# Cross-attention's probabilities x values with three heads per stationary operand, and the last weight's units moved behind the loop

## The chip, the cores and the metric

One core of a Trainium2 chip runs the whole kernel. The metric is the device time of one launch in microseconds; shown are the median and the extremes of three runs, and one further execution that the hardware profiler recorded. The engines are TensorE (PE; PEld is its load of stationary operands), VectorE (DVE), ScalarE (ACT), GpSimd (POOL) and SyncE (SP), whose queue issues nearly all DMAs.

## What is computed

A perceiver block on 64 latent tokens of width 256: cross-attention to 6272 context tokens (32 heads of 8), self-attention with 16 heads of 128 whose weights come as codes times block scales, and a mixture-of-experts FFN.

```python
x = x + xattn(layernorm(x), ctx, Wq, Wk, Wv)         # q and k rms-normalised per head of 8
x = x + attn(layernorm(x), wq, wk, wv, wo, biases)   # w = codes * repeat(scales, 32, axis=0)
x = x + ffn(layernorm(x), gate, shared, experts)     # top 2 of 8 experts, and a shared one
# inside xattn, per head:
scores = einsum('bhnd,bhmd->bhnm', q, k) * 8 ** -0.5
out = einsum('bhnm,bhmd->bhnd', softmax(scores), v)
```

## The kernel before

**The loop.** The context is cut into 49 tiles of 128 tokens. Each engine runs `step` once per tile, with the stages staggered over tiles. For tile t TensorE does `scores(t, half)` for two halves of 16 heads (L736, 16 matmuls, two heads each), then `values(t - 1, half)` (L750), then the keys and values of tile t + 5 (L772, six matmuls with 512 columns in fp32r, as high and low parts). ScalarE takes the exponentials of each half (L394, 128x1024 into `probs`), and the squares, logarithm and power for the keys' norm (L406, L412, L416). VectorE splits the context, sums the squares, copies the values out of PSUM (L544), scales the keys (L552) and writes their parts (L560). GpSimd makes the context's low part (L348) and the keys' last part (L354). There is no maximum in the softmax: the exponentials and, through a column of ones, their sums are accumulated over all tiles in PSUM.

**Probabilities x values.** `v_sb` holds for every pair of heads a stationary operand of 17 columns: 8 + 8 value columns and one column of ones (L327 sets the ones). Its moving operand is the 128 probabilities of the pair (2 heads x 64 tokens), so each product has two useful and two useless quarters. The 16 matmuls of a tile go to four column groups of TensorE in turn (PSUM partitions 0, 32, 64, 96), four 128-column regions each, all in PSUM bank 6. All operands are f32. `pv_done` counts two per tile.

**After the loop.** VectorE copies the 128x512 sums (L567), TensorE transposes them in eight pieces (L781), VectorE takes reciprocals (L569), multiplies by them (L572), adds the residual (L576), and the second layernorm follows (L456 to L471). TensorE fills the time with `keep_busy(16)` (L695), transposes the normalised rows (L687), waits for both `ring_free` semaphores and starts the projections (L793).

**The quantised weights.** Sixteen units of 128x1024: twelve of Wq, Wk, Wv, four of Wo. `load_codes(u)` brings the codes (512 KB, L280) into their final place, `load_scales(u)` the scales (256 KB for the first twelve, L286; 512 KB for Wo's, L289) into a ring of two slots, after `ring_free` says that unit u - 2 has been multiplied. GpSimd's `dequantise(u)` (L340) multiplies in place and increments `ring_free`. With `DEQ = 3`, SP issues one unit every third tile and GpSimd multiplies one every third tile: the sixteenth is in the loop's last steps. TensorE's gate ahead of the projections asks for all of them:

```python
for k in range(RING):
    pe.wait_ge(ring_free[k], UNITS // RING + 1)
```

**SP's queue.** SP goes through one list in order: per step the transposing DMA of a finished tile's keys (`turn`, L277, after `k2_done`), the next context tile (L269), and at their steps a unit's codes and scales; behind the last step `load_round(r)` for the FFN's five rounds (704 KB, L294, and 352 KB, L295), which the last stage waits for (`up_in`, `down_in`).

Of the kernel before, what the change touches and what calls it, by code (L numbers as in the profile page):

```python
# [19 lines left out]
ALU = mybir.AluOpType  # L20
# [86 lines left out]
def wait(engine, semaphore, count):  # L107

    if count is not None:
        engine.wait_ge(semaphore, count)  # L110


def perceiver(nc, x, ctx_t, xwq, xwkv, codes, scales, wo_scales, qkv_bias, bo, gate_w, gate_bias,
              up_w, down_w, eye, expert_ids, pair_heads, out):
    with ExitStack() as stack:
        def sb(name, shape, dt=F32):
            return stack.enter_context(nc.sbuf_tensor(name, shape, dt))
# [41 lines left out]
        v_flat = sb("v_flat", [P, 8 * PAIRS * VW])  # L159
        v_sb = v_flat[:].rearrange("p (s r v) -> p s r v", s=8, r=PAIRS)  # L160
# [18 lines left out]
        o_sb = sb("o_sb", [P, CG * P])  # L179
        o_den = sb("o_den", [N, 2, PAIRS])  # L180
        o_cat = sb("o_cat", [N, PAIRS, 2, XD])
        x1 = sb("x1", [N, D])
        x1b, x2 = q_f, q_sq

# [31 lines left out]
        ps_o = ps[:, 6, :]  # L216
        ps_oT = ps[0:N, 0:2, :].rearrange("p s (r v) -> p s r v", v=CT)
# [41 lines left out]
        @block.sync  # L259
        def _(sp):  # L260
            sp.dma_start(x_sb[:], x).then_inc(ready("x_in"), 16)
            sp.dma_start(wkv_f[:], xwkv).then_inc(ready("wkv_in"), 16)

            def load(t):

                if t >= 4:
                    sp.wait_ge(ctx_hi_done, t - 3)
                    sp.wait_ge(ctx_lo_done, t - 3)
                sp.dma_start(ctx_f[:, t % 4], ctx_t[t]).then_inc(ctx_in[t % 4], 16)  # L269

            def turn(t):

                sp.wait_ge(k2_done, t + 1)
                if t >= 4:
                    sp.wait_ge(scores_mm, 2 * t - 6)
                rows = k12[:, t % 4].rearrange("p r w -> p (r w)")
                sp.dma_start_transpose(kT[:, t % 4], rows).then_inc(keys_in[t % 4], 16)  # L277

            def load_codes(u):
                sp.dma_start(w_all[:, u], codes[:, u]).then_inc(codes_in[u % RING], 16)  # L280

            def load_scales(u):

                sp.wait_ge(ring_free[u % RING], u // RING + 1)
                if u < NQKV:
                    sp.dma_start(s_ring[:, u % RING, 0:512], scales[u].unsqueeze(0).to_broadcast(  # L286
                        [P // NB, NB, 512])).then_inc(scales_in[u % RING], 16)
                else:
                    sp.dma_start(s_ring[:, u % RING], wo_scales[u - NQKV].unsqueeze(0).to_broadcast(  # L289
                        [QB, P // QB, WS])).then_inc(scales_in[u % RING], 16)  # L290

            def load_round(r):

                sp.dma_start(up_sb[:, :, r], up_w[:, :, r]).then_inc(ready("up_in"), 16)  # L294
                sp.dma_start(dn_sb[:, r], down_w[:, r]).then_inc(ready("down_in"), 16)  # L295

            small = ((bias_t[:], qkv_bias), (bo_sb[:], bo.to_broadcast([N, D])), (gate_sb[:], gate_w),
                     (gb_sb[:], gate_bias.to_broadcast([P, E])))

            for t in range(2):  # L300
                load(t)
            sp.dma_start(wq_sb[:], xwq).then_inc(ready("wq_in"), 16)
            for t in range(2, T + LAG):
                if t >= LAG:
                    turn(t - LAG)
                if t < T:
                    load(t)
                u, piece = divmod(t - LAG, DEQ)
                if 0 <= u < UNITS and piece == 0:
                    load_codes(u)  # L310
                if 0 <= u < UNITS and piece == 1:
                    load_scales(u)
                if 2 <= t < 2 + len(small):
                    dst, src = small[t - 2]
                    sp.dma_start(dst, src).then_inc(ready("small_in"), 16)
            for r in range(NR):
                load_round(r)
            sp.wait_ge(ready("y"), 1)
            sp.dma_start(out, x_sb[:]).then_inc(ready("out_written"), 16)
            sp.wait_ge(ready("out_written"), 16)  # L320

        @block.gpsimd
        def _(pool):
            pool.memset(q_room[:, :, PR:RT], 0.0).then_inc(ready("pads"), 1)
            pool.memset(k12[:, :, :, PR:RT], 0.0).then_inc(ready("pads"), 1)
            pool.memset(zeros[:], 0.0).then_inc(ready("zeros"), 1)
            pool.memset(v_sb[:, :, :, VW - 1], 1.0).then_inc(ready("v_ones"), 1)  # L327
            for k in range(RING):
                pool.memset(s_ring[0:1, k, 0:1], 0.0).then_inc(ring_free[k], 1)

            def dequantise(u):

                pool.wait_ge(codes_in[u % RING], (u // RING + 1) * 16)
# [36 lines left out]
        def _(act):  # L370
# [105 lines left out]
        def _(dve):  # L476
# [48 lines left out]
            def step(t):  # L525
# [9 lines left out]
                if r.exists():  # L535
# [6 lines left out]
                    wait(dve, kv_mm, r.count(plus=1))  # L542
                    wait(dve, pv_done, r.count(2, -10))
                    nc.vector.tensor_copy(  # L544
                        v_sb[:, r.slot(8), :, 0:2 * XD],
                        ps_kv[r.slot(2)][:, D:2 * D].rearrange("p (r v) -> p r v", v=2 * XD)).then_inc(v_done, 1)
                if r.exists():

                    kn = k_n[:, r.slot(2)].rearrange("p (h d) -> p h d", d=XD)
# [19 lines left out]
            nc.vector.reciprocal(o_den[:], ps_oT[:, :, :, VW - 1]).then_inc(ready("o_den"), 1)  # L569
            dve.wait_ge(ready("o_den"), 1)  # L570
            for h in range(2):
                nc.vector.tensor_tensor(  # L572
                    o_cat[:, :, h, :], ps_oT[:, h, :, h * XD:(h + 1) * XD],
                    o_den[:, h].unsqueeze(2).to_broadcast([N, PAIRS, XD]), ALU.mult).then_inc(ready("o_cat"), 1)
            dve.wait_ge(ready("o_cat"), 2)
            nc.vector.tensor_tensor(x1[:], x_sb[:], o_cat[:].rearrange("p r h d -> p (r h d)"), ALU.add).then_inc(  # L576
                ready("x1"), 1)
            dve.wait_ge(ready("x1"), 1)
            layernorm_dve(dve, "ln2", x1[:])
# [102 lines left out]
        def _(pe):  # L682
# [58 lines left out]
            def values(t, half):  # L741

                wait(pe, exp_done, t.count(2, half + 1))
                if half == 0:
                    wait(pe, v_done, t.count(plus=1))
                for k in range(PAIRS // 2):
                    r = half * PAIRS // 2 + k
                    j, g = r % CG, r // CG
                    at = k % 2 * 512 + k // 2 * P
                    last = nc.tensor.matmul(ps_o[CT * j:CT * j + VW, g * P:(g + 1) * P], v_sb[:, t.slot(8), r],  # L750
                                            probs[:, t.slot(2), half, at:at + P], start=False,
                                            stop=False, skip_group_check=True)
                last.then_inc(pv_done, 1)

            def step(t):
                pv, kv = t.ahead(PV), t.ahead(PROJ)
                for half in range(2):
                    if t.exists():
                        scores(t, half)
                for half in range(2):  # L760
                    if pv.exists():
                        values(pv, half)
                if kv.exists():

                    wait(pe, ctx_lo_done, kv.count(plus=1))
# [8 lines left out]

            steps(pe, step, {-4: queries_mm, -2: queries_turned})

            pe.wait_ge(ready("o_sb"), 1)
            for h in range(2):
# [205 lines left out]
```

## Time and profile before

| | us |
|---|---|
| median of 3 runs | 229.02 |
| lowest, highest | 227.82, 229.48 |
| profiled execution | 227.25 |
| its span, first to last instruction | 225.4 |

A row of the chain of waits or of the timeline begins with its start and its length in us; a matmul's end is modelled, so short matmuls overlap in it. A merged row gives the count as x16. The granted clock is the share of 2.4 GHz that TensorE was given: 1.00 is 2.4 GHz, 0.50 is 1.2 GHz. Lines are those of the kernel before.

### The profile page before, as it was taken

Reading aid. Unit: us, or ns where it says so; the run is one execution under the profiler, and the core shown is the slowest. Engines: PE = TensorE matmul, PEld = TensorE weight load, DVE = VectorE, ACT = ScalarE, POOL = GpSimd, SP = SyncE. Lnnn points to the kernel's source line nnn. Section 1 sums busy time; section 2 is a strip of 40 time slices with the busy share of each in tenths; the row PEclk is TensorE's granted clock in tenths of the full one; section 3 lists DMA queues with packets and bytes.
Section 4 is the critical chain, followed back from the end, with each engine's and each line's share of the span. In section 5 each row is a group of like instructions: output and inputs, shape, how many; then the busy total and the mean of one; then the engine's idle time right before and its main releaser. Section 6 shows DMA issues by size and latency. Waiting matters only on the chain.

```text
span 225.4 us, 7792 instructions
## 1 busy us (share of the span) xinstructions
PE 203.5 (90%) x2964; PEld 136.9 (61%) x2964; DVE 131.5 (58%) x332; ACT 144.6 (64%) x277; POOL 106.4 (47%) x124
## 2 busy tenths in 40 slices
PE   0594899999999999999999999999977889988994
PEld 0362677777776777767777777777745533563442
DVE  3448656776667767677676775767740432744721
ACT  3023578888888988889888888888888212413230
POOL 3214446585765857757577575776728000000000
PEclk9999799999999999999999999999999999999999
DMA  5313999999998998989899998999999997000000
GB/s 173 129 43 75 265 200 190 167 216 228 240 200 207 203 221 209 199 213 192 217 224 186 224 203 205 265 202 241 149 289 214 293 280 233 20 3 0 0 3 12
DMA packets 66672, 39.63 MB, mean 176 GB/s; under 512 B 53991, under 2 KB 60583, under 8 KB 66655
## 3 DMA queue, kind: packets, MB, share of 16 engines
q1 hardware_dynamic: 66223, 39.34, 78.0%
q8 instruction: 10, 0.16, 0.3%
q10 hardware_dynamic: 432, 0.07, 0.2%
q14 instruction: 7, 0.06, 0.1%
HBM read 26.49 MB, written 0.07 MB: 118 GB/s over the span
## 4 chain that ended last, share of the span: by engine, by line
PE 82%; DVE 7%; DMA 5%; ACT 2%; issue 2%; POOL 1%; SPq 0%; DVEq 0%; ACTq 0%
PE ps L772 34%; PE ps L750 20%; PE ps L736 11%; PE ps L793 5%; DMA kT<-k 3%; PE ps L882 3%; PE ps L898 2%; DMA wkv_f<-xwkv 2%; PE ps L844 2%; PE ps L802 1%; PE ps L832 1%; PE ps L890 1%; ACT room L394 1%; DVE k_n L552 1%; DVE wkv_lo L486 1%
## 5 line engine op out<-in xcount | busy, mean ns | idle before, releaser
L394 ACT ACTIVATE room<-ps 128x1024 f32<-128x1024 f32 x98 | 100.2, 1029 | 22.3 <-PE ps L736 22.3
L348 POOL TENSOR_TENSOR ctx_lo<-ctx_f,ctx_hi 128x256 fp32r<-128x256 f32 x49 | 35.8, 732 | 62.1 <-DVE ctx_hi L533 62.1
L750 PE MATMUL ps<-room,v_flat 128*17 128x128 f32 x1568 | 52.3, 274 | 0.0
L772 PE MATMUL ps<-wkv_hi,ctx_hi 128*128 128x512 f32 x98 | 45.2, 462 | 4.4 <-DVE q_blk L522 2.4
L750 PEld LDWEIGHTS ps<-room,v_flat 128*17 128x17 f32 x1568 | 38.6, 97 | 5.3 <-ACT room L394 0.3
L772 PE MATMUL ps<-wkv_lo,ctx_hi 128*128 128x512 f32 x98 | 40.0, 408 | 0.0
L772 PE MATMUL ps<-wkv_hi,ctx_lo 128*128 128x512 f32 x98 | 40.0, 408 | 0.0
L560 DVE CAST k<-k_n 128x512 f16<-128x512 f32 x49 | 36.8, 751 | 2.6
L340 POOL TENSOR_TENSOR w_all<-w_all,s_ring 128x1024 f32<-128x1024 f32 x16 | 37.9, 2373 | 0.0
L552 DVE TENSOR_TENSOR k_n<-ps,k_r 128x256 f32<-128x256 f32 x49 | 20.8, 424 | 24.9 <-ACT k_r L416 24.9
L736 PEld LDWEIGHTS ps<-q_blk,kT 48*128 48x128 f16 x784 | 22.4, 95 | 21.2 <-issue 13.4
L354 POOL TENSOR_TENSOR k<-k_n,k 128x256 f16<-128x256 f32 x49 | 33.0, 674 | 4.8 <-DVE k L560 4.8
L736 PE MATMUL ps<-q_blk,kT 48*128 48x128 f16 x784 | 31.4, 219 | 3.1 <-ACT room L394 1.6
L539 DVE TENSOR_REDUCE k_ss<-k_sq 128x32 f32<-128x256 f32 x49 | 20.3, 415 | 21.4 <-ACT k_sq L406 21.3
L772 PEld LDWEIGHTS ps<-wkv_hi,ctx_hi 128*128 128x128 f32 x98 | 19.1, 195 | 17.4 <-issue 10.6
L406 ACT ACTIVATE k_sq<-ps 128x256 f32<-128x256 f32 x49 | 18.5, 378 | 7.9 <-PE ps L772 7.9
L772 PEld LDWEIGHTS ps<-wkv_hi,ctx_lo 128*128 128x128 f32 x98 | 19.2, 196 | 4.8
L772 PEld LDWEIGHTS ps<-wkv_lo,ctx_hi 128*128 128x128 f32 x98 | 19.3, 197 | 2.4
L544 DVE COPY v_flat<-ps 128x256 f32<-128x256 f32 x49 | 20.2, 412 | 0.0
L412 ACT ACTIVATE k_ln<-k_ss,eps_rms 128x32 f32<-128x32 f32 x49 | 16.1, 328 | 5.9 <-DVE k_ss L539 5.7
L533 DVE CAST ctx_hi<-ctx_f 128x256 fp32r<-128x256 f32 x49 | 13.8, 284 | 3.9 <-PE ps L772 3.8
L416 ACT ACTIVATE k_r<-k_ln 128x32 f32<-128x32 f32 x49 | 11.3, 230 | 1.5
(111 smaller groups left out, 115.1 us busy)
## 6 DMA issues: line engine op xcount, KB each, us to landing
w_all<-codes SPq DMA_DIRECT2D x16, 512.0 KB, 4.3
ctx_f<-ctx_t SPq DMA_DIRECT2D x49, 128.0 KB, 3.0
up_sb<-up_w SPq DMA_DIRECT2D x5, 704.0 KB, 10.5
s_ring<-scales SPq DMA_DIRECT2D x12, 256.0 KB, 3.8
s_ring<-wo_scales SPq DMA_DIRECT2D x4, 512.0 KB, 5.3
dn_sb<-down_w SPq DMA_DIRECT2D x5, 352.0 KB
kT<-k SPq DMA_TRANSPOSE x49, 3.5
wkv_f<-xwkv SPq DMA_DIRECT2D x1, 512.0 KB, 4.4
```

The costliest lines, as they stand in the source:

```text
L340: nc.gpsimd.tensor_tensor(w, w, s, ALU.mult).then_inc(ring_free[u % RING], 1)
L348: nc.gpsimd.tensor_tensor(ctx_lo[:, split.slot(2)], ctx_f[:, split.slot(4)], ctx_hi[:, split.slot(2)].bitcast(F32), ALU.subtract).then_inc ...
L354: nc.gpsimd.tensor_tensor(key_part(keys, 2), k_n[:, keys.slot(2)].rearrange("p (r h d) -> p r h d", h=2, d=XD), key_part(keys, 0), ALU.sub ...
L394: nc.scalar.activation(probs[:, t.slot(2), half], ps_scores[half].rearrange("p b n -> p (b n)"), ACT.Exp).then_inc(exp_done, 1)
L406: nc.scalar.activation(k_sq[:, a], ps_kv[a][:, 0:D], ACT.Square).then_inc(sq_done, 1)
L539: nc.vector.tensor_reduce(k_ss[:, r.slot(2)], k_sq[:, r.slot(2)].rearrange("p (h d) -> p h d", d=XD), AX_X, ALU.add).then_inc(ss_done, 1)
L544: nc.vector.tensor_copy(v_sb[:, r.slot(8), :, 0:2 * XD], ps_kv[r.slot(2)][:, D:2 * D].rearrange("p (r v) -> p r v", v=2 * XD)).then_inc(v_ ...
L552: nc.vector.tensor_tensor(kn, ps_kv[r.slot(2)][:, 0:D].rearrange("p (h d) -> p h d", d=XD), k_r[:, r.slot(2)].unsqueeze(2).to_broadcast([P ...
L560: nc.vector.tensor_copy(key_parts(r)[:, :, :, 0:2, :], pairs.unsqueeze(3).to_broadcast([P, PAIRS, 2, 2, XD])).then_inc(k1_done, 1)
L736: last = nc.tensor.matmul(ps_scores[half][:, e, at:at + P], kT[rows, t.slot(4), r // 2], q_blk[rows, r // 2].rearrange("p h n -> p (h n)") ...
L750: last = nc.tensor.matmul(ps_o[CT * j:CT * j + VW, g * P:(g + 1) * P], v_sb[:, t.slot(8), r], probs[:, t.slot(2), half, at:at + P], start= ...
L772: last = nc.tensor.matmul(ps_kv[a], lhs, rhs, start=(n == 0), stop=(n == len(terms) - 1))
```

## The change

**Values.** A stationary operand now holds three heads (two in the last group) of nine columns each, eight values and a column of ones: 27 or 18 columns. The moving operand is those heads' probabilities, 192 or 128 columns. `values` runs in three groups of four matmuls, one per column group: heads by slot 0 to 11, 12 to 23, and 24 to 31. Twelve matmuls a tile take the place of sixteen. The second group straddles the two halves of the exponentials; `pv_done` still counts two per tile, after groups 1 and 2. The sums lie in bank 6 (384 columns) and bank 7 (128). The heads are put in an order that suits this by permuting the rows of Wq, Wk and Wv on the host.

**After the loop.** VectorE copies the first 384 columns after group 1, ScalarE the last 128 after group 2; eight f32 matmuls against chosen columns of the identity replace the eight transposes, and one multiply replaces two.

**Weight units.** `DEQ` goes from 3 to 4, and only the first twelve units are loaded and multiplied within the loop. Wo's four are loaded behind the last `turn`, mixed with the FFN's rounds, and multiplied by GpSimd behind its loop. The gate ahead of the projections is not touched.

```diff
-VW = 2 * XD + 1
+VW = XD + 1
+TRIO = 3
+GROUPS = ((0, 0, TRIO), (TRIO * CG, TRIO, TRIO), (2 * TRIO * CG, 2 * TRIO, 2))
+POS = XH // CG
-DEQ0, DEQ = 3, 3
+DEQ0, DEQ = 3, 4
...
                 u, piece = divmod(t - LAG, DEQ)
-                if 0 <= u < UNITS and piece == 0:
+                if 0 <= u < NQKV and piece == 0:
                     load_codes(u)
-                if 0 <= u < UNITS and piece == 1:
+                if 0 <= u < NQKV and piece == 1:
                     load_scales(u)
...
+            for u in range(NQKV, NQKV + RING):
+                load_codes(u)
+                load_scales(u)
+            for u in range(NQKV + RING, UNITS):
+                load_codes(u)
             for r in range(NR):
                 load_round(r)
+                if r < UNITS - NQKV - RING:
+                    load_scales(NQKV + RING + r)
...
-            pool.memset(v_sb[:, :, :, VW - 1], 1.0).then_inc(ready("v_ones"), 1)
+            pool.memset(v_sb[:, :, :, XD], 1.0).then_inc(ready("v_ones"), 1)
...
                 u, piece = divmod(c - DEQ0, DEQ)
-                if 0 <= u < UNITS and piece == 0:
+                if 0 <= u < NQKV and piece == 0:
                     dequantise(u)
+            for u in range(NQKV, UNITS):
+                dequantise(u)
...
+            act.wait_ge(pv_done, 2 * T)
+            nc.scalar.activation(o_sb[:, 2 * TRIO:POS].rearrange("p a n -> p (a n)"), ps_o[1], ACT.Copy).then_inc(
+                ready("o_pairs"), 1)
...
-            dve.wait_ge(pv_done, 2 * T)
-            nc.vector.tensor_copy(o_sb[:], ps_o).then_inc(ready("o_sb"), 1)
+            dve.wait_ge(pv_done, 2 * T - 1)
+            nc.vector.tensor_copy(o_sb[:, 0:2 * TRIO].rearrange("p a n -> p (a n)"), ps_o[0]).then_inc(
+                ready("o_trios"), 1)
...
-            nc.tensor.matmul(ps_o, zeros[:, 0:P], zeros[:], start=True, stop=True, skip_group_check=True)
+            for sums in ps_o:
+                nc.tensor.matmul(sums, zeros[:, 0:P], zeros[:, 0:sums.shape[1]], start=True, stop=True,
+                                 skip_group_check=True)
...
+            def values(t, group):
+
+                first, at, heads = GROUPS[group]
+                if group < 2:
+                    wait(pe, exp_done, t.count(2, group + 1))
+                if group == 0:
                     wait(pe, v_done, t.count(plus=1))
...
+                at = at % (2 * TRIO) * N
+                moving = probs[:, t.slot(2)].rearrange("p h n -> p (h n)")
+                for j in range(CG):
+                    slot = first + heads * j
+                    last = nc.tensor.matmul(ps_o[group // 2][CT * j:CT * j + heads * VW, at:at + heads * N],
+                                            v_sb[:, t.slot(8), slot:slot + heads].rearrange("p h v -> p (h v)"),
+                                            moving[:, slot * N:(slot + heads) * N], start=False, stop=False,
+                                            skip_group_check=True)
+                if group > 0:
+                    last.then_inc(pv_done, 1)
...
-            for h in range(2):
-                for g in range(CG):
-                    at = g * P + h * N
-                    last = nc.tensor.transpose(ps[0:N, h, g * P:(g + 1) * P], o_sb[:, at:at + N], ident[:])
+            pe.wait_ge(ready("o_trios"), 1)
+            pick = ident[:].rearrange("p (j v) -> p j v", v=CT)
+            for at in range(POS):
+                if at == 2 * TRIO:
+                    pe.wait_ge(ready("o_pairs"), 1)
+                own = at % TRIO * VW
+                last = nc.tensor.matmul(ps_oT[:, at * CG:(at + 1) * CG], o_sb[:, at], pick[:, :, own:own + VW],
+                                        start=True, stop=True, skip_group_check=True)
```

## Rows read from the trace of the kernel before

**Rows 1.** The page: TensorE in the busy table; the values matmuls among the groups

```profile
PE 203.5 (90%) x2964; PEld 136.9 (61%) x2964; DVE 131.5 (58%) x332; ACT 144.6 (64%) x277; POOL 106.4 (47%) x124
...
L750 PE MATMUL ps<-room,v_flat 128*17 128x128 f32 x1568 | 52.3, 274 | 0.0
```

**Rows 2.** Chain of waits (start, length, what), one tile of the loop

```profile
157.56 0.55 PE ps L736 x16
158.11 1.00 PE ps L750 x32
159.11 1.60 PE ps L772 x6
```

**Rows 3.** Timeline, weight loads of the values matmuls and of the projections

```profile
101.56 0.12 PEld L750 LDWEIGHTS ps<-room,v_flat 128*17 128x17 f32 x4
...
101.88 0.12 PEld L750 LDWEIGHTS ps<-room,v_flat 128*17 128x17 f32 x4
...
183.62 0.14 PEld L793 LDWEIGHTS ps<-w_all,hT 128*64 128x64 f32 x2 [0.28 <-issue]
184.05 0.14 PEld L793 LDWEIGHTS ps<-w_all,hT 128*64 128x64 f32 x2 [0.28 <-issue]
```

**Rows 4.** Groups from 101 to 148 us: busy, mean ns, idle before by releaser

```profile
L394 ACT ACTIVATE room<-ps 128x1024 f32<-128x1024 f32 x30 | 30.9, 1030 | 6.6 <-PE ps L736 6.6
```

**Rows 5.** Timeline (in brackets idle before, releaser), last five tiles

```profile
164.35 0.62 PE L736 MATMUL ps<-q_blk,kT 48*128 48x128 f16 x16 [0.50 <-DMA kT<-k]
...
171.67 0.62 PE L736 MATMUL ps<-q_blk,kT 48*128 48x128 f16 x16 [0.93 <-DMA kT<-k]
172.11 3.77 ACT L394 ACTIVATE room<-ps 128x1024 f32<-128x1024 f32 x4 [1.00 <-PE ps L736]
```

**Rows 6.** Timeline of SP's queue, issues at the end of the loop

```profile
161.56 0.58 SPq L280 DMA_DIRECT2D w_all<-codes  x1
...
164.74 0.59 SPq L289 DMA_DIRECT2D s_ring<-wo_scales  x1
165.46 4.93 SPq L277 DMA_TRANSPOSE kT<-k  x2
170.44 0.58 SPq L294 DMA_DIRECT2D up_sb<-up_w  x1
```

**Rows 7.** Line 294, the FFN rounds' first piece: issues, and time to landing

```profile
L294 SPq DMA_DIRECT2D up_sb<-up_w x5: 546/560/992, 170.4 to 175.5; - x5
...
DMA to landing us min/median/max: 5.2/10.5/16.1
```

**Rows 8.** Stretches: engines' busy times, clock, DMA share, GB/s (last column)

```profile
172.00:184.00 12.00, 9.85 (x154) 5.85 (x150) 4.34 (x14) 4.27 (x6) 1.77 (x1) 1.00 1.01 294
...
182.00:184.00 2.00, 1.19 (x6) 0.54 (x8) 0.90 (x3) 0.00 (x0) 0.00 (x0) 1.00 1.05 337
```

**Rows 9.** Line 340, GpSimd's multiplication: ns min/median/max, first and last start

```profile
L340 POOL TENSOR_TENSOR w_all<-w_all,s_ring x16: 2360/2373/2384, 37.5 to 171.4; 128x1024 f32<-128x1024 f32 x16
```

**Rows 10.** Chain of waits behind the loop; the L695 row is the timeline's

```profile
176.64 0.70 DVE o_sb L567
177.38 1.08 PE ps L781 x8
...
178.28 3.62 PE L695 MATMUL ps<-zeros 128*128 128x512 f16 x16
...
183.14 3.65 PE ps L793 x16
...
209.22 3.60 PE ps L882 x24
```

**Rows 11.** Early TensorE: chain of waits, and a stretch with its clock (0.50)

```profile
9.28 5.46 PE ps L772 x12
...
25.94 2.68 PE ps L772 x6
...
24.90:28.20 3.30, 3.30 (x23) 2.59 (x22) 1.38 (x4) 2.62 (x5) 1.36 (x3) 0.50 1.15 262
```

More of the change, by code:

```diff
@@ L158, in perceiver @@
         k12 = sb("k12", [P, 4, PAIRS, RT], F16)
-        v_flat = sb("v_flat", [P, 8 * PAIRS * VW])
-        v_sb = v_flat[:].rearrange("p (s r v) -> p s r v", s=8, r=PAIRS)
+        v_sb = sb("v_sb", [P, 8, XH, VW])
         kT = sb("kT", [P, 4, KC, P], F16)
@@ L178, in perceiver @@
         q_room = sb("q_room", [N, PAIRS, RT], F16)
-        o_sb = sb("o_sb", [P, CG * P])
-        o_den = sb("o_den", [N, 2, PAIRS])
-        o_cat = sb("o_cat", [N, PAIRS, 2, XD])
+        o_sb = sb("o_sb", [P, POS, N])
+        o_den = sb("o_den", [N, XH])
+        o_cat = sb("o_cat", [N, XH, XD])
         x1 = sb("x1", [N, D])
@@ L215, in perceiver @@
         ps_kv = [ps[:, 4, :], ps[:, 5, :]]
-        ps_o = ps[:, 6, :]
-        ps_oT = ps[0:N, 0:2, :].rearrange("p s (r v) -> p s r v", v=CT)
+        ps_o = [ps[:, 6, 0:2 * TRIO * N], ps[:, 7, 0:2 * N]]
+        ps_oT = ps[0:N, 0, 0:XH * VW].rearrange("p (r v) -> p r v", v=VW)
         ps_qk = [[ps[:, 0, :], ps[:, 2, :]], [ps[:, 1, :], ps[:, 3, :]]]
@@ L279, in load_codes @@
             def load_codes(u):
-                sp.dma_start(w_all[:, u], codes[:, u]).then_inc(codes_in[u % RING], 16)
+                sp.dma_start(w_all[:, u], codes[:, u]).then_inc(
+                    codes_in[u % RING] if u < NQKV else ready(f"wo_codes{u}"), 16)
             def load_scales(u):
@@ L331, in dequantise @@
             def dequantise(u):
-                pool.wait_ge(codes_in[u % RING], (u // RING + 1) * 16)
+                if u < NQKV:
+                    pool.wait_ge(codes_in[u % RING], (u // RING + 1) * 16)
+                else:
+                    pool.wait_ge(ready(f"wo_codes{u}"), 16)
                 pool.wait_ge(scales_in[u % RING], (u // RING + 1) * 16)
@@ L544, in step @@
                     nc.vector.tensor_copy(
-                        v_sb[:, r.slot(8), :, 0:2 * XD],
-                        ps_kv[r.slot(2)][:, D:2 * D].rearrange("p (r v) -> p r v", v=2 * XD)).then_inc(v_done, 1)
+                        v_sb[:, r.slot(8), :, 0:XD],
+                        ps_kv[r.slot(2)][:, D:2 * D].rearrange("p (h d) -> p h d", d=XD)).then_inc(v_done, 1)
                 if r.exists():
@@ L563, in _ @@
             steps(dve, step, {-4: queries_squared, -3: queries_split, -2: queries_placed})
-            dve.wait_ge(pv_done, 2 * T)
-            nc.vector.tensor_copy(o_sb[:], ps_o).then_inc(ready("o_sb"), 1)
+            dve.wait_ge(pv_done, 2 * T - 1)
+            nc.vector.tensor_copy(o_sb[:, 0:2 * TRIO].rearrange("p a n -> p (a n)"), ps_o[0]).then_inc(
+                ready("o_trios"), 1)
             dve.wait_ge(ready("oT_cross"), 1)
-            nc.vector.reciprocal(o_den[:], ps_oT[:, :, :, VW - 1]).then_inc(ready("o_den"), 1)
+            nc.vector.reciprocal(o_den[:], ps_oT[:, :, XD]).then_inc(ready("o_den"), 1)
             dve.wait_ge(ready("o_den"), 1)
-            for h in range(2):
[L572 to L576, printed above, removed]
+            nc.vector.tensor_tensor(o_cat[:], ps_oT[:, :, 0:XD], o_den[:].unsqueeze(2).to_broadcast([N, XH, XD]),
+                                    ALU.mult).then_inc(ready("o_cat"), 1)
+            dve.wait_ge(ready("o_cat"), 1)
+            nc.vector.tensor_tensor(x1[:], x_sb[:], o_cat[:].rearrange("p h d -> p (h d)"), ALU.add).then_inc(
                 ready("x1"), 1)
@@ L739, in scores @@
                 last.then_inc(scores_mm, 1)
-            def values(t, half):
-                wait(pe, exp_done, t.count(2, half + 1))
-                if half == 0:
-                    wait(pe, v_done, t.count(plus=1))
[L746 to L753, printed above, removed]
+            def values(t, group):
[3 more added lines that the diff above has]
+                if group == 0:
+                    wait(pe, v_done, t.count(plus=1))
+                at = at % (2 * TRIO) * N
[8 more added lines that the diff above has]
+                    last.then_inc(pv_done, 1)
             def step(t):
@@ L759, in step @@
                         scores(t, half)
-                for half in range(2):
+                for group in range(len(GROUPS)):
                     if pv.exists():
-                        values(pv, half)
+                        values(pv, group)
                 if kv.exists():
@@ L930, in rows @@
         return w.reshape(NB, DC, P // NB, w.shape[1]).transpose(2, 0, 1, 3).reshape(P, DC, w.shape[1])
+    by_slot = [CG * (at + i) + j for _, at, heads in GROUPS for j in range(CG) for i in range(heads)]
+    pairs = [half * PAIRS // 2 + k % 2 * (PAIRS // 4) + k // 2 for half in range(2) for k in range(PAIRS // 2)]
+    by_pair = [by_slot[2 * r + h] for r in pairs for h in range(2)]
     wkv = np.concatenate([np.asarray(L0_xattn_Wk), np.asarray(L0_xattn_Wv)])
-    wkv = wkv.reshape(XH, XD, 2, D).transpose(2, 0, 1, 3).reshape(2 * D, D)
+    wk, wv = wkv.reshape(XH, XD, 2, D).transpose(2, 0, 1, 3)
+    wkv = np.concatenate([wk[by_pair], wv[by_slot]]).reshape(2 * D, D)
+    wq = np.asarray(L0_xattn_Wq).reshape(XH, XD, D)[by_pair].reshape(D, D)
     def v_cols(w):
@@ L958 @@
         "ctx_t": np.asarray(ctx_2048).reshape(T, P, DC, P).transpose(0, 3, 2, 1),
-        "xwq": rows(np.asarray(L0_xattn_Wq).T),
+        "xwq": rows(wq.T),
         "xwkv": wkv.T.reshape(DC, P, 2 * D).transpose(1, 0, 2),
```

2 lines of the change are left out of this document (removed).

## The prediction

> **What bounds the kernel now.** I read the page's busy table first. TensorE is busy 90% of the span [rows 1]. That alone doesn't say it sets the end, so the chain of waits came next. In the loop over the 49 context tiles it never leaves TensorE: scores 0.55 us, probabilities x values 1.00 us, keys and values 1.60 us, 3.15 us a tile [rows 2]. So in the loop only TensorE's time counts. ScalarE is the next limit: over 47 us (15 tiles) its exponentials waited 6.6 us for scores, 0.44 us a tile [rows 4]. The loop could become that much shorter and no more.
>
> After the loop the order is different: the sums are copied, turned, normalised, and the projections begin at 183.14 [rows 10]. TensorE goes through two gates there, the second layernorm and the two `ring_free` counts in front of `project`. Those ask for all 16 weight units. Before, the last two were multiplied by 173.8 [rows 9], nine microseconds ahead of the layernorm, so this gate is invisible. The change makes it visible, I think.
>
> **The values matmuls.** Per tile, 16 matmuls of 128 columns become 8 of 192 and 4 of 128, each recorded twice since f32 goes in two passes (1568 records [rows 1] for 49 x 16 = 784 matmuls). In each column group that is 4 x 128 = 512 columns before and 192 + 192 + 128 = 512 after. What is the price: columns or instructions? The weight loads show the beat. Groups of four start at 101.56 and, three groups on, at 101.88 [rows 3]: 0.11 us a round of four column groups. The projections, f32 with 512 columns, load their pair every 0.43 us [rows 3]: four times the columns, four times the beat. So columns pay. A line through the two gives (0.43 - 0.11)/384 = 0.83 ns a column, hence 0.16 us for 192 columns. A tile: before 8 rounds x 0.11 = 0.88; after 4 x 0.16 + 2 x 0.11 = 0.86 to 0.88. I take 0.01 us a tile, 0.3 us over the loop (0.0 to 1.0). The wider stationary operand (27 columns for 17) is loaded during the round before, which gets longer too; if it showed, it would be a few ns for each of 6 rounds, under 1.5 us over 49 tiles. Keep both ends: -1.0 to +1.5, value -0.3.
>
> The values copy moves as many elements as before, the ones' memset doubles at the start while GpSimd waits, and a second zeroing matmul appears: 0.
>
> **The loop's DMAs.** A unit every fourth tile for every third, and 12 for 16. TensorE waits for no DMA in the steady loop, so this gives nothing there. It gives something in the last tiles. Transposes of keys queued behind weight pieces came late: scores waited 0.50 us at 164.35 and 0.93 us at 171.67, and ScalarE's exponentials then 1.00 us [rows 5]. In the queue, codes went out at 161.56 and 512 KB of scales at 164.74, right ahead of the last two transposes [rows 6]. After, the last loads in the loop are codes 11 (four steps ahead of the last transpose) and 256 KB of scales 11. I let both stalls go: 0.5 + 1.0 = 1.5 us off the end of the loop (0.5 to 1.5). The last transpose's issue moves only by the first stall and the loop's gain, since the second stall comes after its keys are made: 0.5 + 0.3 = 0.8, some 0.9 with the relieved queue.
>
> **The end of attention.** The 0.70 us copy becomes 384 columns on VectorE and 128 on ScalarE; the last tile's group 1 now needs the second half of the exponentials. Eight turns (1.08 us [rows 10]) become eight matmuls in two passes, 16 loads of 64 columns: from 1.1 to 2.2 us. Together -0.3 to +1.0. All this ends well ahead of the gate below and costs nothing while the gate holds. Uncovered, it stands against the 1.5 us.
>
> **The last four units.** This is the term that counts. SP issues in order: last transpose, codes 12, scales 12, codes 13, scales 13 (after unit 11 is multiplied), codes 14, codes 15, round 0 of the FFN weights (1056 KB), scales 14, round 1, scales 15, rounds 2 to 4. Each unit is 512 KB of codes and 512 KB of scales. Ahead of the landing of scales 15 stand 4 x 1024 KB + 2 x 1056 KB = 6208 KB = 6.36 MB.
>
> Does one transfer wait for another? The five rounds in this trace were issued 170.4 to 175.5 and landed 5.2 to 16.1 us after issue [rows 7]: first landing 175.6, last 191.6, one round per 4.0 us. They landed in turn, at the rate of the engines. At 4.0 us per round the first 704 KB take 2.7 us, so the stream began at 173.0. After the change it begins at 172.1.
>
> Rate: 294 GB/s from 172 to 184, 337 in its best two microseconds [rows 8]; by the landings 270. I take 294, because the weight units fill all 128 partitions where the later, slower part of the rounds fills 88. 6.36 MB / 0.294 = 21.6 us: scales 15 at 193.7. The two waits of SP (scales 14 for unit 12, scales 15 for unit 13) end near 178 and 182 by 2.4 us a multiplication [rows 9], while the queue holds work to 186 and later: nothing starves. Unit 15 is multiplied in 2.4 us: gate open at 196.1. Before, projections began at 183.1: **+13.0 us**. At 337 GB/s from 171.6 the gate opens at 192.9 (+9.8); at 270 from 173.0 at 199.0 (+15.9).
>
> The Trainium skill ("DMA: Bandwidth & Descriptors", Specifications) gives about 358 GB/s as one core's limit to HBM. No stretch of two microseconds in this trace shows it; by it the 6.36 MB take 17.8 us and the wait is an estimated 9 us.
>
> **The clock.** `keep_busy` ended at 181.9 [rows 10]; TensorE then has nothing for some 14 us. In this trace, after an idle stretch of 2.4 us near 21 to 23, the granted clock was 0.50 (1.2 GHz) from 24.9 to 28.2, and six key/value matmuls took 2.68 instead of 1.6 us [rows 11, 2]: 1.5 us lost. The projections run back to back, 16 in 3.65 us at full clock [rows 10]. If the half clock lasts as it did there, they lose about 1.6. The first twelve key/value matmuls of the kernel, after a long idle start, took 5.46 us [rows 11], where two tiles cost 3.2 at full clock: up to 2.7 with the matmuls around them. I take 2.1 (1.5 to 2.7).
>
> **Behind it.** Rounds 2 to 4 land some 12 us after scales 15, near 206. The up projections began at 209.2 [rows 10] and move to 224: no second wait.
>
> **Sum.** Gate +13.0, clock +2.1; the loop's 1.8 us count only through the earlier start, already in. 225.4 + 15.1 = 240.5 span; around the span the profiled run has 227.25 - 225.4 = 1.85: 242.4 us. Its own time is 1.8 under the runs' median of 229.02, so on the median it would be 244; I say 242.5.
>
> **Rivals.**
> *The queue is faster or slower than 294 GB/s.* Not another mechanism, the size of the same one: 225.4 + 9.8 + 1.5 + 1.85 = 238.6, to 225.4 + 15.9 + 2.7 + 1.85 = 245.9, or 247.6 on the median.
> *The gate is hidden.* If the 6.36 MB and the last multiplication are through by 182, only the gains remain: 227.25 - 1.8 + 0.3 = 225.8, faster. It needs 6.36 MB in 182 - 2.4 - 172.1 = 7.5 us, 850 GB/s; [rows 8] speak against it. Even if the scales' broadcast cost nothing, the other 4.26 MB need 14.5 us. Chance 3%.
> *Matmuls are paid by the instruction.* 1.00 us / 32 records = 31 ns; eight records fewer save 0.25 us a tile, within ScalarE's slack, 12.3 us over the loop. The gate moves as early: 242.4 - 12.3 = 230.1, about no change. For it: only the mean. Against it: the beat of [rows 3]. Chance 3%. The Trainium skill ("TensorEngine Tiling (Array Packing)", Instruction Overhead) has such a rule, some 60 cycles for each matmul: at 2.4 GHz an estimated 25 ns x 8 = 0.2 us a tile, 9.8 us. By that rule it would be about 232.6.
> *Wider loads show.* With 1.5 us more in the loop: 244.2, inside the range. 4%.
>
> **Chances.** The gate holds as worked out 90%. Slower by over 1% 0.94; within 1% (what a measurement of this kernel can just tell) 0.03; faster 0.03. Range 237.5 to 247.5.
>
> **What would show it.** Right: GpSimd's last four multiplications far apart, the last ending near 196; projections' first matmul behind it; granted clock 0.5 for some microseconds after; the values stage still near 1.00 us a tile at a 3.14 us beat; no long wait for the last keys; up projections not waiting. Wrong: a tile under 3.0 us; the last multiplication before 183; the scales landing out of turn.

## The result, and the profile after

| | before | changed |
|---|---|---|
| median | 229.25 us (227.82 to 229.94, 4 runs) | 243.03 us (242.85 to 243.92, 4 runs) |
| span of the profiled execution | 225.4 us | 241.2 us |
| projections start in it | 183.14 us | 197.28 us |

The ratio of the times is 1.0617, with a 95% interval from 1.0559 to 1.0675: the changed kernel is slower by 6.2%. The prediction was 242.5 us, from 237.5 to 247.5.

The chain of waits of the changed kernel, one tile of the loop and then the way to the projections (start, length, what; lines are the changed kernel's: L755 scores, L771 values, L795 keys and values, L819 projections):

```profile
157.03 0.55 PE ps L755 x16
157.58 1.00 PE ps L771 x24
158.58 1.60 PE ps L795 x6
...
171.96 6.75 DMA s_ring<-wo_scales
...
178.84 2.35 POOL w_all L353
...
181.20 13.46 DMA s_ring<-wo_scales
...
194.77 2.38 POOLq L118
...
197.28 5.30 PE ps L819 x16
```

A tile looks like the one of [rows 2], with 24 records in the values stage for 32. Behind the loop the chain no longer goes through the layernorm: it goes through the scales' DMAs. The longest piece, 13.46 us, is scales 15 on its way through the queue.

The timeline of the same kernel, GpSimd's last four multiplications (in brackets the idle time before, and what ended it) and TensorE's next work:

```profile
175.42 2.35 POOL L353 TENSOR_TENSOR w_all<-w_all,s_ring 128x1024 f32<-128x1024 f32 x1 [5.05 <-DMA s_ring<-wo_scales]
178.84 2.34 POOL L353 TENSOR_TENSOR w_all<-w_all,s_ring 128x1024 f32<-128x1024 f32 x1 [1.07 <-DMA s_ring<-wo_scales]
188.49 2.34 POOL L353 TENSOR_TENSOR w_all<-w_all,s_ring 128x1024 f32<-128x1024 f32 x1 [7.31 <-DMA s_ring<-wo_scales]
194.80 2.34 POOL L353 TENSOR_TENSOR w_all<-w_all,s_ring 128x1024 f32<-128x1024 f32 x1 [3.97 <-DMA s_ring<-wo_scales]
...
181.48 0.33 PE L704 MATMUL ps<-ident,h_sb 64*128 64x64 f32 x2 [1.74 <-DVE h_sb L489]
197.28 3.58 PE L819 MATMUL ps<-w_all,hT 128*64 128x512 f32 x8 [15.47 <-POOL w_all L353]
```

TensorE turned the normalised rows at 181.48, almost a microsecond earlier than before, and then stood still for 15.47 us until the sixteenth unit was multiplied. The multiplication itself takes what it did [rows 9]; it starts late because its scales land late.

The stretches around it (length; busy time of PE, PEld, DVE, ACT, POOL with counts; granted clock, DMA share, GB/s):

```profile
172.00:184.00 12.00, 7.49 (x90) 4.16 (x90) 5.53 (x13) 2.58 (x5) 4.69 (x2) 0.98 0.99 342
184.00:196.00 12.00, 0.00 (x0) 0.00 (x0) 0.00 (x0) 0.00 (x0) 3.54 (x2) 0.50 1.03 281
197.20:202.60 5.40, 5.32 (x17) 1.69 (x18) 0.00 (x0) 0.60 (x1) 0.00 (x0) 0.68 0.72 202
```

The queue is full throughout, and TensorE does nothing at a granted clock of 0.50. When its work returns the clock averages 0.68, and the 16 projections take 5.30 us against 3.65 [rows 10].

### The profile page after: what moved, and what is told of

Same layout as the page of the kernel before. It is cut to its first block, busy times and chain, and to the rows that moved or that the text cites. A ratio compares the mean times of both kernels' runs of the same rounds, so it can differ in the third digit from the quotient of the medians.

```text
span 241.2 us, 7026 instructions
## 1 busy us (share of the span) xinstructions
PE 205.0 (85%) x2581; PEld 129.9 (54%) x2581; DVE 129.2 (54%) x331; ACT 144.7 (60%) x278; POOL 106.6 (44%) x124
## 4 chain that ended last, share of the span: by engine, by line
PE 75%; DMA 9%; DVE 6%; issue 3%; POOL 2%; ACT 2%; SPq 2%; POOLq 1%; DVEq 0%; ACTq 0%
PE ps L795 32%; PE ps L771 17%; PE ps L755 10%; DMA s_ring<-wo_scales 8%; PE ps L819 5%; PE ps L908 3%; PE ps L924 2%; PE ps L870 2%; POOLq L118 1%; POOL w_all L353 1%; DMA x_sb<-x 1%; PE ps L828 1%; PE ps L858 1%; SPq L282 1%; PE ps L916 1%
## 5 line engine op out<-in xcount | busy, mean ns | idle before, releaser
L771 PE MATMUL ps<-room,v_sb 128*27 128x192 f32 (+1 forms) x1176 | 52.5, 312 | 0.1
L795 PE MATMUL ps<-wkv_hi,ctx_hi 128*128 128x512 f32 x98 | 45.1, 460 | 4.4 <-DVE q_blk L540 2.4
L795 PE MATMUL ps<-wkv_lo,ctx_hi 128*128 128x512 f32 x98 | 39.9, 407 | 0.0
L795 PE MATMUL ps<-wkv_hi,ctx_lo 128*128 128x512 f32 x98 | 39.7, 405 | 0.0
L771 PEld LDWEIGHTS ps<-room,v_sb 128*27 128x27 f32 (+1 forms) x1176 | 31.2, 103 | 12.9 <-ACT room L409 0.5
L578 DVE CAST k<-k_n 128x512 f16<-128x512 f32 x49 | 32.6, 666 | 2.6
L755 PEld LDWEIGHTS ps<-q_blk,kT 48*128 48x128 f16 x784 | 22.4, 95 | 19.8 <-issue 14.1
L755 PE MATMUL ps<-q_blk,kT 48*128 48x128 f16 x784 | 31.6, 219 | 1.5 <-ACT room L409 1.3
L795 PEld LDWEIGHTS ps<-wkv_hi,ctx_hi 128*128 128x128 f32 x98 | 19.0, 193 | 17.4 <-issue 10.5
L819 PE MATMUL ps<-w_all,hT 128*64 128x512 f32 x48 | 13.0, 677 | 15.5 <-POOL w_all L353 15.5
L795 PEld LDWEIGHTS ps<-wkv_hi,ctx_lo 128*128 128x128 f32 x98 | 19.1, 195 | 4.7
L795 PEld LDWEIGHTS ps<-wkv_lo,ctx_hi 128*128 128x128 f32 x98 | 19.2, 196 | 2.4
L562 DVE COPY v_sb<-ps 128x256 f32<-128x256 f32 x49 | 20.2, 413 | 0.0
```

Source lines behind the costliest of these rows:

```text
L562: nc.vector.tensor_copy(v_sb[:, r.slot(8), :, 0:XD], ps_kv[r.slot(2)][:, D:2 * D].rearrange("p (h d) -> p h d", d=XD)).then_inc(v_done, 1)
L578: nc.vector.tensor_copy(key_parts(r)[:, :, :, 0:2, :], pairs.unsqueeze(3).to_broadcast([P, PAIRS, 2, 2, XD])).then_inc(k1_done, 1)
L755: last = nc.tensor.matmul(ps_scores[half][:, e, at:at + P], kT[rows, t.slot(4), r // 2], q_blk[rows, r // 2].rearrange("p h n -> p (h n)") ...
L771: last = nc.tensor.matmul(ps_o[group // 2][CT * j:CT * j + heads * VW, at:at + heads * N], v_sb[:, t.slot(8), slot:slot + heads].rearrange ...
L795: last = nc.tensor.matmul(ps_kv[a], lhs, rhs, start=(n == 0), stop=(n == len(terms) - 1))
L819: last = nc.tensor.matmul(dst[b * N:(b + 1) * N], hT[:, c, :], w_all[:, 3 * (2 * b + s) + w, c * 512:(c + 1) * 512], start=(c == 0), stop= ...
```

## The experiments

The theory: the whole loss is the gate ahead of the projections, which waits for bytes in queue order, and the half clock behind it. The rivals: the new values part costs (or gains) something itself; the wait is GpSimd's chain and not the queue; the slow projections come from the DMA traffic. Times of before, run beside them on the same chip: 228.37 us for the first four, 228.38 for the next four, 227.69 for the last two; the changed kernel's 243.03 was taken beside a before of 229.25, so a difference between two groups is uncertain by about a microsecond.

**The values part alone.** The changed kernel with before's loads.

```diff
-DEQ0, DEQ = 3, 4
+DEQ0, DEQ = 3, 3
...
-                if 0 <= u < NQKV and piece == 0:
+                if 0 <= u < UNITS and piece == 0:
```

(the same at the scales and at `dequantise`; the units behind the loop go.)

> The new values matmuls and the new end of attention, with all sixteen weight units loaded and multiplied inside the loop as before. If columns set the price of the values matmuls, a tile stays at 3.14 to 3.15 us and the time is that of before within 1% (227.5 to 229.5 us); the late transposes of the last keys come back, about 1.5 us over the changed kernel's loop end. Rival, a price by the matmul: 0.2 to 0.25 us a tile less, 217 to 220 us.

226.67 us, ratio 0.9952 (0.9903 to 1.0002): no difference that these runs resolve, though the median lies 0.8 us below the range that was expected. The price by the matmul (217 to 220 us) is out. As expected the last keys are late again; its timeline, the scores of the last but one tile:

```profile
171.38 0.62 PE L742 MATMUL ps<-q_blk,kT 48*128 48x128 f16 x16 [1.30 <-DMA kT<-k]
```

**The loads alone.** The kernel before, with only the loads and multiplications of the change.

```diff
+            for u in range(NQKV, NQKV + RING):
+                load_codes(u)
+                load_scales(u)
...
+            for u in range(NQKV, UNITS):
+                dequantise(u)
```

> The old values matmuls, with only the loads and multiplications moved as the change moves them. If the gate ahead of the projections carries the whole loss, this is as slow as the changed kernel: 242 to 244 us, the last multiplication ending near 197, and TensorE idle some 14 us. If part of the loss comes from the new values part, it lies below 241 us.

242.64 us, ratio 1.0695 (1.0576 to 1.0813). The loss is the loads' alone. Its gate opened just ahead of 193.99 in the profiled execution (stretches first, then the timeline):

```profile
172.00:184.00 12.00, 7.32 (x98) 4.34 (x98) 5.98 (x14) 2.33 (x5) 4.69 (x2) 0.93 1.02 365
184.00:192.00 8.00, 0.00 (x0) 0.00 (x0) 0.00 (x0) 0.00 (x0) 2.83 (x2) 0.50 1.03 357
```

```profile
193.99 6.34 PE L806 MATMUL ps<-w_all,hT 128*64 128x512 f32 x16 [11.65 <-POOL w_all L351]
```

The same bytes in the same order went at 357 to 365 GB/s here and at 281 to 342 in the changed kernel's profile. The queue's rate differs from execution to execution, and with it the gate, by three microseconds. Why it differs is open. The 16 projections took 6.34 us here, at a granted clock of 0.57, against 5.30 in the changed kernel: what the clock costs differs between executions too.

**The units ahead of the FFN rounds.**

```diff
-            for u in range(NQKV, NQKV + RING):
+            for u in range(NQKV, UNITS):
                 load_codes(u)
+                if u < NQKV + RING:
+                    load_scales(u)
+            for u in range(NQKV + RING, UNITS):
                 load_scales(u)
-            for u in range(NQKV + RING, UNITS):
-                load_codes(u)
             for r in range(NR):
                 load_round(r)
-                if r < UNITS - NQKV - RING:
-                    load_scales(NQKV + RING + r)
```

> The changed kernel with the last two scales issued ahead of all FFN rounds. If the gate waits for bytes in queue order, two rounds of 1056 KB less stand ahead: the last scales land near 184 and the gate opens near 186.5 instead of 197.2. Time 230.5 us if the clock stays at its full level over the some 4 us of idleness, 232.2 us if it falls. Rival, that the wait is GpSimd's chain of four multiplications and SP's waits between them: the gate opens only one or two us earlier, 241 us.

234.64 us, 8.4 us less than the changed kernel. The bytes ahead are most of the wait, but the gain is 2.4 us short of the forecast for a clock that falls, and it did fall (16 projections in 5.04 us): the gate opened at 189.2, not at 186.5. The timeline shows why, GpSimd first and then SP's queue:

```profile
176.95 2.34 POOL L352 TENSOR_TENSOR w_all<-w_all,s_ring 128x1024 f32<-128x1024 f32 x1 [5.67 <-DMA s_ring<-wo_scales]
180.19 2.34 POOL L352 TENSOR_TENSOR w_all<-w_all,s_ring 128x1024 f32<-128x1024 f32 x1 [0.89 <-DMA s_ring<-wo_scales]
184.28 4.77 POOL L352 TENSOR_TENSOR w_all<-w_all,s_ring 128x1024 f32<-128x1024 f32 x2 [1.76 <-DMA s_ring<-wo_scales]
...
173.52 1.29 SPq L282 DMA_DIRECT2D w_all<-codes  x2
179.32 3.77 SPq L292 DMA_DIRECT2D s_ring<-wo_scales  x2
```

Scales 14 could be issued only at 179.32, when unit 12 was multiplied, and by then the queue had little left: the DMA share from 172 to 184 was 0.84, against 0.99 in the changed kernel. Scales 14 then took 4.8 us to land, and the last two multiplications ran back to back to 189.05. So the rival was right for the rest: with the rounds out of the way, the ring of two slots and GpSimd's chain set the end.

**The gate split.** The loads as the change has them.

```diff
             for k in range(RING):
-                pe.wait_ge(ring_free[k], UNITS // RING + 1)
+                pe.wait_ge(ring_free[k], NQKV // RING + 1)
...
             pe.wait_ge(pT_out, 2)
+            for k in range(RING):
+                pe.wait_ge(ring_free[k], UNITS // RING + 1)
             join_heads(0)
```

> The changed kernel with its loads as they are, and the gate split: ahead of the projections TensorE asks for the twelve units of Wq, Wk and Wv, and for all sixteen only ahead of the output projection. The last multiplication (near 197) would be done 3 us before the output projection starts (near 200), so the whole loss goes: 226.3 us by the spans, up to 228 if GpSimd's multiplications slow VectorE's work beside them. If instead another cost of the change than the gate is at work, it stays above 230 us.

227.99 us, ratio to before 0.9981 (0.993 to 1.0033): the loss is gone, with no byte less and no DMA moved. Wo's units are not needed before the output projection. The run is at the upper end of what was expected; its chain of waits:

```profile
177.15 1.50 DVE x L593
...
181.97 5.35 PE ps L819 x16
```

VectorE's residual add, 0.43 us in the kernel before, takes 1.50. TensorE's filling matmuls run out at 179.84, 1.41 us before the layernorm is done (0.52 in the kernel before), and the 16 projections run at a granted clock of 0.68 on average: 5.35 us for 3.65. In the changed kernel all this lay under the gate.

**The gate split, and GpSimd waits for the layernorm.**

```diff
+            pool.wait_ge(ready("ln2_h"), 1)
             for u in range(NQKV, UNITS):
                 dequantise(u)
```

> The split gate, and GpSimd begins the last four multiplications only after the second layernorm's output is written. If it is GpSimd's multiplications that stretched VectorE's residual add to 1.50 us (0.43 before) and let TensorE run out of idle work, then the add is back at 0.43, projections start at 181 instead of 182 and take 3.65 instead of 5.35 us: 2.8 us under the split gate alone, near 225 us. Unit 15 ends near 198.7, before the output projection. Rival, that VectorE's stretch comes from the DMA traffic: no change.

225.80 us, ratio 0.9891 (0.9829 to 0.9952), 2.2 us under the split gate alone. Chain of waits, then the timeline:

```profile
177.11 0.43 DVE x L594
...
180.86 3.65 PE ps L820 x16
```

```profile
194.94 2.35 POOL L353 TENSOR_TENSOR w_all<-w_all,s_ring 128x1024 f32<-128x1024 f32 x1 [3.71 <-DMA s_ring<-wo_scales]
...
195.41 2.16 DVE L627 TENSOR_TENSOR room<-room,s_inv 128x256 f32<-128x256 f32 x1
```

The add is back at 0.43 and the projections at 3.65, while the DMAs go on as before (391 GB/s from 176 to 181, 406 under the split gate alone): it was GpSimd's multiplication. The last one now meets VectorE elsewhere: a multiply of two SBUF operands that takes 0.42 us alone takes 2.16 and ends 0.3 us behind it. That stretch delays TensorE (1.01 us idle), the granted clock averages 0.68 from 199.7 to 205, and this execution's output projection took 5.32 us, against 3.63 in the kernel before. With 227.7 us it was the slowest of the six, so the median need not contain this.

**TensorE kept at work in the wait.** The changed kernel with filling matmuls ahead of the gate, 62 in one run and 72 in the other.

```diff
             transpose_h("ln2")
+            keep_busy(62)
```

> The changed kernel with 62 idle-time matmuls (some 13.4 us) between the second layernorm's transposes and the gate, so that TensorE waits about 2 us instead of 15 with nothing to do. If the half clock behind the gate costs what the trace of the changed kernel shows (16 projections in 5.30 us against 3.65), these 1.6 us go and the gate stays near 197: 241.3 us by the changed kernel's 243.0. Rival, that the slow projections come from loads still running in the queue: no change, 243 us.

> As the run with 62 filling matmuls, but with 72 (15.5 us), so that TensorE works until the gate opens, near 197.3. With 62 it stood still for 3.6 us in the profiled execution and the clock fell again. Expected: granted clock 1.00 through the projections, 16 of them in 3.65 us, and a time of 241.2 to 241.5 us in all executions. Rival, as before: projections as slow as in the changed kernel because of the loads still running, 243 us.

242.60 us with 62; two executions at 241.2 and 241.3, as expected, and the others at 242.6, 245.8 and 246.9: undecided. In the profiled execution (245.8) the gate opened at 199.1, 3.6 us after the last filling matmul, and the clock had fallen: 16 projections in 6.28 us. With 72 TensorE worked until the gate opened. Its chain of waits:

```profile
182.94 17.40 PE ps L712 x72
200.40 3.65 PE ps L820 x16
```

and the stretch behind the gate:

```profile
198.60:206.00 7.40, 7.34 (x37) 2.75 (x34) 0.69 (x1) 1.19 (x2) 1.65 (x1) 1.00 0.67 200
```

The projections run at 1.00 in 3.65 us while rounds 2 to 4 still load at 200 GB/s, so the traffic is not what slowed them. From the gate to the end of the span it takes 242.7 - 200.4 = 42.3 us, as in the kernel before (225.4 - 183.1 = 42.3), and 43.9 in the changed one (241.2 - 197.3): the clock costs 1.6 us there.

The clock had not held all the way. VectorE's writing of the normalised rows took 1.72 us beside a multiplication of GpSimd (0.52 without), TensorE stood still for 2.27 us ahead of 182.22, and among the filling matmuls the granted clock was down at 0.50:

```profile
184.00:187.00 3.00, 3.00 (x8) 1.06 (x7) 0.00 (x0) 0.00 (x0) 0.00 (x0) 0.50 1.05 264
190.00:200.40 10.40, 10.34 (x49) 4.54 (x47) 0.00 (x0) 0.00 (x0) 4.69 (x2) 1.00 0.95 241
```

So the 72 took 17.40 us instead of 15.5, and they ended together with the gate. The median, 243.57 (ratio to before 1.0601, the changed kernel's 1.0617), shows no gain. In the profiled execution scales 15 landed at 197.8, against 194.7, and the last multiplication ended three microseconds later. But filling matmuls that start at 182.9 and need 15.5 us also keep TensorE until 198.4, a microsecond past the changed kernel's gate. Which of the two held the other executions up is not shown. The expected 241.2 was reached by one of four. That the gate's scatter covers the clock's 1.6 us was not foreseen.

**Fewer columns, as many matmuls.** In the 40 tiles of the rolled loop each values matmul streams 32 columns fewer, and the sums of those tiles leave out half of each last head's tokens.

```diff
+                    wide = heads * N - (0 if t.i is None else N // 2)
...
-                                            moving[:, slot * N:(slot + heads) * N], start=False, stop=False,
+                                            moving[:, slot * N:slot * N + wide], start=False, stop=False,
```

> The changed kernel, in which each values matmul of the 40 tiles of the rolled loop streams 32 columns fewer (160 for 192, 96 for 128; half of each last head's tokens is left out of those tiles' sums), with the same number of matmuls. If columns are the price at 0.83 ns each, a tile loses 6 rounds x 32 x 0.83 ns = 0.16 us, 6.4 us over the 40 tiles, and the gate comes as much earlier: 236.6 us. If matmuls are paid by the piece: 243 us.

236.94 us (two executions), for 236.6 expected. Chain of waits:

```profile
102.62 0.55 PE ps L755 x16
103.17 0.84 PE ps L772 x24
104.02 1.60 PE ps L796 x6
105.61 0.55 PE ps L755 x16
```

The values stage falls from 1.00 to 0.84 us and the tile from 3.15 to 2.99: 0.16 us, as the line through the two beats of [rows 3] gives. The gate opens at 190.88 instead of 197.28, the 6.4 us that were expected. Columns are the price.

**The units earlier in the loop.** All sixteen in the loop, one every third tile, three steps earlier; once with the new values part, once in the kernel before (whose edit is shown).

```diff
+EARLY = 3
-DEQ0, DEQ = 3, 3
+DEQ0, DEQ = 0, 3
...
-                u, piece = divmod(t - LAG, DEQ)
+                u, piece = divmod(t - LAG + EARLY, DEQ)
```

> The new values matmuls with all sixteen units inside the loop, one every third tile, but loaded and multiplied three steps earlier than before, so that the last scales are out of the queue before the last five transposes. Expected: no wait for the last keys and no multiplication beside the layernorm: 1.3 to 1.5 us under the values-only kernel, 225.2 us where that had 226.7. Rival, that the extra 768 KB a unit so early delay the first tiles' loads: same or slower.

> The kernel before with only the weight units moved three steps earlier (all sixteen in the loop, one every third tile). If the gain of the same move with the new values matmuls is the loads' alone, this lies 1.3 to 1.5 us under the kernel before, 226.9 us beside 228.4, and the new values part and end of attention are worth the rest, 0.5 to 2 us. If the gain needs the new values matmuls, no change from before.

224.82 us with the new values part, ratio 0.9855 (0.980 to 0.991); 225.02 us with the old one, ratio 0.9874 (0.9825 to 0.9924). Both beat the kernel before. The first beats both kernels and is the fastest of the study; over the second it has 0.2 us, which the intervals do not separate. The gain is the loads' alone. It was forecast at 1.3 to 1.5 us from the late keys and came out at 2.7 in the old kernel, and the 0.5 to 2 us that were expected of the new values part did not come. SP's queue in the first of them:

```profile
155.39 0.60 SPq L292 DMA_DIRECT2D s_ring<-wo_scales  x1
156.17 12.92 SPq L280 DMA_TRANSPOSE kT<-k  x5
169.14 0.58 SPq L297 DMA_DIRECT2D up_sb<-up_w  x1
```

The last scales leave at 155.39 and five transposes follow with nothing between them; no scores wait for keys. The profiled executions take the gain with the old values part apart. Its projections start at 180.62 instead of 183.14, 2.5 us earlier. Of this 0.9 us is there by the middle of the loop, where a values stage starts at 100.56 instead of 101.50 with the same beat, and 1.6 us arises at the loop's end, as forecast. The early part lies in the first tiles, where the kernel before had the clock's dip of [rows 11] and this execution a granted clock of 1.00 from 24 to 34 us; whether that belongs to the earlier units or to the execution is not shown.

## Why the prediction was right

**The loop.** The step was that columns and not matmuls are paid. The changed kernel's own tile, the values-only run and the run with fewer columns all say so. The forecast of 0.01 us gained a tile has the wrong sign, though. The chain of waits of the changed kernel:

```profile
100.82 1.00 PE ps L771 x24
...
157.58 1.00 PE ps L771 x24
```

and of the kernel with the old values part and the earlier units:

```profile
100.56 1.00 PE ps L751 x32
...
160.32 1.00 PE ps L751 x32
```

18 tiles in 56.76 us are 3.153 us each, 19 tiles in 59.76 us are 3.145: the new tile is 8 ns longer, 0.4 us over the loop. That lies within the ends that were kept (-1.0 to +1.5 us); that the wider loads are its cause was not tried. The rule of the Trainium skill ("TensorEngine Tiling (Array Packing)", Instruction Overhead), weighed as a rival, would have given 9.8 us here, if its 60 cycles are added to every matmul, as the prediction read it; for these matmuls of 96 to 192 columns the trace disagrees. The same section says that a matmul with one column takes as long as one with 60: read so, as a least duration, the rule touches none of them, and the trace agrees.

**The gate.** The step that carried the number was the sum over the queue: 6.36 MB at 294 GB/s from 172.1, scales 15 at 193.7, gate at 196.1. They landed at 194.7 and the gate opened at 197.2: 14.1 us for 13.0. Scales 12 to 15 landed in their order. That the number is so close is partly luck, because more was moved than counted, and faster. The rate was 342 GB/s for twelve microseconds and 281 for the next twelve, more than forecast on average; from the issue of codes 12 to the landing of scales 15 it was 303:

```profile
169.36:194.67 25.31, 9.84 (x150) 5.50 (x142) 5.53 (x13) 5.22 (x8) 8.04 (x4) 0.78 1.00 303
```

But 303 GB/s over 25.31 us are 7.7 MB, where the prediction counted 6.36. The last transpose, issued just before, accounts for an estimated 0.3 of the difference (what the queue's 39.3 MB leave for its 49 transposes). Some megabyte of the FFN rounds that stand behind scales 15 had then moved before scales 15 had landed; in the loads-only run, 339 GB/s over 22.04 us, it is much the same. The scales landed in the queue's order, but the bytes moved by then were more than those ahead of them. And the rate is no constant: with the same loads the other runs' gates lay between 194.0 and 200.4. The two waits of SP were forecast to starve nothing, and they didn't as long as the rounds stood between (the run with the units first shows what they cost otherwise). The limit of some 358 GB/s that the Trainium skill gives ("DMA: Bandwidth & Descriptors", Specifications), and that I said no stretch of the first trace showed, was passed: 365 GB/s over twelve microseconds in the loads-only run, 406 over five under the split gate. The same page says in its section on bandwidth that each core gets roughly this figure when both cores of a memory domain stream, and gives 425 GB/s for a large load by one core; here one core runs alone, so it was no limit for this kernel.

**The clock.** Forecast 2.1 (1.5 to 2.7), measured 1.6 in the changed kernel's trace (5.30 against 3.65, and the same by the rest of the span), as the rows of the first dip gave. The dearer figure from the cold start was not wrong either: behind their gates the 16 projections took 6.34 us in the loads-only run, 6.28 with 62 filling matmuls and 6.35 with fewer columns, 2.6 to 2.7 us lost. The time that TensorE had stood still does not order them: 15.5 us in the changed kernel, 11.7 in the loads-only run, 3.6 with 62. With the units first it was 5.04 us, 1.4 lost. So 2.1 was about the middle of what occurs, and what decides between its ends stays open.

**The end of the loop.** The stalls for the last keys went, as forecast: the last transpose was issued at 168.08 against 169.16 before, 1.08 us earlier for 0.9. It counts only through the queue's start.

**What was covered.** The eight f32 matmuls in place of the transposes took 1.12 us against 1.06, by the timeline, at the lower end of 1.1 to 2.2. What the working did not have is GpSimd's multiplications beside the layernorm. They cost nothing under the gate, and over 2 us once it was split. A forecast for the split gate made by the same steps alone would have been wrong by that much: whoever moves work to an engine has to ask what it does to its neighbour, also where it is off the path.

**The sum.** Span +15.8 us for +15.1 (14.1 + 1.7 for 13.0 + 2.1). The errors are of opposite sign.

## What to carry to other kernels

A gate that asks for all of a ring's units is harmless while all of them are early; when loads are moved, look for every counter that they feed and ask for each unit only where it is first read. To price a late load, sum the bytes ahead of it in its queue, and give the rate a range of a fifth to either side. Matmuls spread over column groups were paid by their columns at 96 to 192 columns each, so packing heads into fewer instructions with the same columns buys nothing here.

## What was not expected of the hardware

GpSimd's 128x1024 multiplication stretches VectorE's work on SBUF: the residual add 0.43 to 1.50 us, the writing of the normalised rows 0.52 to 1.33 and once 1.72, a 128x256 multiply 0.42 to 2.16, each ending 0.2 to 0.3 us behind the multiplication where the two meet. In the changed kernel's timeline, beside the multiplication of 175.42 to 177.77 and that of 178.84 to 181.18:

```profile
177.06 0.98 DVE L593 TENSOR_TENSOR x<-x_sb,o_cat 64x256 f32<-64x256 f32 x1
...
180.09 1.33 DVE L489 TENSOR_SCALAR h_sb<-x,mv,rs 64x256 f32<-64x256 f32 x1
```

Not all of VectorE's work is stretched. The 64x256 product of `o_cat`, which reads PSUM, kept its 0.42 us at 176.61, beside the first of these multiplications. Under the split gate the layernorm's statistics over the same rows in SBUF kept their 0.42 us at 178.67, beside the multiplication of 178.58 to 180.93. The Trainium skill ("SBUF — State Buffer", SBUF: two separate sides) describes it: the two engines share a pair of ports, held for a whole instruction by whichever starts first, and of VectorE's instructions only those with two inputs in SBUF or in a mode that uses two ports need it. The runs agree as far as they go.

The trace of the kernel before has such a row already, a cast of the keys that takes 0.43 us elsewhere and here ends 0.28 us behind GpSimd:

```profile
159.99 2.37 POOL L340 TENSOR_TENSOR w_all<-w_all,s_ring 128x1024 f32<-128x1024 f32 x1
161.10 1.54 DVE L560 CAST k<-k_n 128x512 f16<-128x512 f32 x1
```

The prediction could have drawn on it.

From the issue of codes 12 (near 169.4 in each) to the landing of scales 15, the same loads took 22.0 us in the loads-only run, 25.3 in the changed kernel and 28.2 with 72 filling matmuls: a scatter between executions larger than most of what was measured here. It costs time where something waits for the queue.
